# One pipeline for the mixture and the delay screen, with the last stage's weights and coefficients made inside it

## The chip, the cores and the metric

The kernel runs on one core of a Trainium2 chip. The metric is the device time of one execution, in microseconds. An execution is one launch; the profile is one execution more, with its span taken from the first to the last instruction.

## The reference, cut to what matters

The input has 16 samples of 64 channels by 2048 points. A convolution front end turns it into h, 16 tiles of 128 rows by 1024. Four blocks follow, each on a layer norm of h (no gain or bias) and each added to h: attention, a mixture of eight rank-16 experts, the delay average, and a dense layer with eight gated rank-16 adapters.

```python
h = h + attention(layernorm(h))
# mixture: the best expert by x @ route_w.T, weighted by its logit
h = h + out                      # (one_hot * logit * (x @ A)) @ Bw
# delay average, x = layernorm(h)
f = rfft(x); corr = irfft(f * conj(f), n=1024)
weights, delay = top_k(corr, 6)
h = h + sum_k softmax(weights)[k] * x[(i + delay[k]) % 1024]
# dense: x = layernorm(h)
h = h + x @ W.T + b + combined   # combined: softmax over experts of q.k / sqrt(32)
```

The correlation at lag 0 of a normalised row is 1024. Where it leads all other lags by enough, the softmax gives it all the weight in float32, and the delay average of the row is the row itself: h becomes h + layernorm(h). A screen proves this bound for all rows or lets the whole average run.

## The kernel before, in words

h stays in SBUF the whole time (16 tiles, 128x1024 f32). Conv and attention come first and are not touched; attention leaves the coefficients rstd and shift of the mixture's layer norm for tiles 0 to 11. From then on (`middle_stages`, L2064) each stage is a block of its own: all engines meet at its end, and `prime` (L78) opens the semaphores of the next.

**Mixture** (`mixture_stage`, L1361). A loop over 16 tiles on four engines. ACT normalises tile t+2 (L1234) and copies the transposed tile t+1 from PSUM (L1250). PE projects tile t onto 128 adapter rows and 8 logits (L1482, f32), transposes tile t+1 (L1242), makes the output product of tile t-1 (L1474), and transposes the weighted projection wh (L1493). DVE picks the expert in small linked steps (`route_of`, L1432 to L1442) and adds the product to h (L1450). It also takes the statistics of tiles 12 to 15 within the first group. POOL only rounds the screen's tables (L1324); SP loads them.

**Screen** (`screen`, L1504). Again 16 tiles, in four quarters. ACT normalises a row by coefficients taken from h (`ScreenStats`, L1327, a chain of linked steps per quarter on DVE). DVE folds it to sum and difference of its halves (L1558, L1559), PE transposes both (L1643), ACT rounds them (L1604). Per quarter there are four units of a real transform (`dft`, L1657: 8 products of 512 columns each, f32r, two for even and two for odd frequencies), ACT squares real and imaginary parts (L1612), POOL adds them (L1632), PE transforms back to lags 1 to 512 (`correlate`, L1669) and DVE takes each tile's largest (L1565). The smallest lead over all rows against NO_WEIGHT = 150 sets dl_flag (L1587). SP loads qka and bm in this block.

**Delay stage** (`delay_stage`, L1821). Each engine reads the flag. If it is 0, the full average runs (`delay_average`, L1696). Else DVE multiplies ten tiles by 1 + rstd and adds shift (L1857), and ACT does six (L1867).

**Last stage** (`final_stage`, L1876). f32 products are made of three f32r ones, so each weight is split into a rounded high part (ACT, `Weight.high`, L1282) and the rest (`Weight.low`, L1288; POOL has qka and half of w, DVE the other half of w and bm). w has 8 chunks of 1024 columns, qka 5, bm 1. DVE takes the statistics of four tiles at a time (L1145) and makes coefficients in a chain (L1157 to L1161); ACT normalises (L1170) and casts (L1186), DVE makes the low part (L1192). PE does q and k (L2008 to L2010 with qp, ka), waits for w and bm (`ready`), and does the output groups. POOL adds the bias to h (L1929), DVE the product (L1986), SP stores.

What sets the order everywhere is the program order of each engine, written out by hand, with semaphore waits. `Links` (L46) joins small DVE steps: each waits for the one before it.

## Time and profile before

| what | value |
| --- | --- |
| median of 3 runs | 2971.6 us (2968.55 to 2972.6) |
| span of the profiled execution | 2970.8 us, 37847 instructions |
| mean granted TensorE clock | 0.966 of full |
| mixture, screen (in the trace) | 2403.3 to 2493.8, to 2596.0 |
| last stage's block | from 2607.45 to the end |

The page gives no own time of the profiled execution beside its span; the median of the runs is 0.8 us above the span. Times in the trace count from the first instruction. A row of the timeline gives start, length, engine, line and operation; equal neighbours are merged (x16), and the length then runs from the first start to the last end. A matmul's length holds the time until its result is out, so the distance of two starts is the better price. f32 matmuls show as two records each.

### The profile page before, as it was taken

How to read it: one execution, taken by the hardware profiler on the slowest of the kernel's cores; microseconds unless marked ns; L12 is line 12 of the kernel's file. 1: busy time of each engine (PE TensorE's matmuls, PEld its weight loads, DVE VectorE, ACT ScalarE, POOL GpSimd, SP SyncE). 2: the span in 40 equal slices, each digit the busy share in tenths (PEclk: the TensorE clock that was granted, in tenths of full speed). 3: DMA queues.
4: the chain of work that ended last, by engine and by line, in shares of the span. 5: the costliest groups of instructions: out<-in, count | busy, mean ns of one | idle time of the engine just before them, and what ended most of it. 6: DMA issues, size and time to landing. Idle time of an engine off the chain costs nothing. (4 is left out here: it accounts for less than half of the span.)

```text
span 2970.8 us, 37847 instructions
## 1 busy us (share of the span) xinstructions
PE 2775.2 (93%) x13321; PEld 2304.8 (78%) x13321; DVE 1865.8 (63%) x3357; ACT 1003.5 (34%) x2026; POOL 129.9 (4%) x76
## 2 busy tenths in 40 slices
PE   7994899999999999999999999999999887759999
PEld 6772788888788888878888887888888765548888
DVE  4887666667766665777666667766666557462331
ACT  3542333333433333333333333333333334431110
POOL 2110000000000000000000000000000000241100
PEclk9996899999999999999999999999999898879999
DMA  4320322223222222222222222222222111010000
GB/s 110 76 63 0 108 79 78 77 78 94 69 93 79 78 78 78 92 71 88 85 78 78 78 90 66 94 85 78 78 78 92 43 58 43 1 71 29 22 28 29
DMA packets 55469, 207.19 MB, mean 70 GB/s; under 512 B 6784, under 2 KB 7168, under 8 KB 53312
## 3 DMA queue, kind: packets, MB, share of 16 engines
q1 hardware_dynamic: 55360, 205.79, 22.3%
q8 instruction: 63, 1.03, 0.1%
q14 instruction: 46, 0.38, 0.0%
HBM read 197.37 MB, written 8.39 MB: 69 GB/s over the span
## 5 line engine op out<-in xcount | busy, mean ns | idle before, releaser
L1013 PE MATMUL at_proj<-qr_xhi,at_whi 128*128 128x512 f32 x1536 | 615.7, 401 | 11.7 <-DVE at_wlo L884 7.1
L1015 PE MATMUL at_proj<-qr_xhi,at_wlo 128*128 128x512 f32 x1536 | 601.5, 392 | 0.0
L1014 PE MATMUL at_proj<-qr_xlo,at_whi 128*128 128x512 f32 x1536 | 600.0, 391 | 0.0
L754 ACT CAST at_ohi<-at_ov 128x512 fp32r<-128x512 f32 x128 | 75.1, 587 | 847.9 <-PE at_ov L1042 847.9
L1013 PEld LDWEIGHTS at_proj<-qr_xhi,at_whi 128*128 128x128 f32 x1536 | 289.7, 189 | 68.7 <-DVE at_wlo L884 7.7
L1015 PEld LDWEIGHTS at_proj<-qr_xhi,at_wlo 128*128 128x128 f32 x1536 | 289.3, 188 | 63.6
L1014 PEld LDWEIGHTS at_proj<-qr_xlo,at_whi 128*128 128x128 f32 x1536 | 290.2, 189 | 56.7
L1060 PE MATMUL at_out<-at_wohi,at_ohi 128*128 128x512 f32 x1008 | 311.6, 390 | 4.0 <-DVE at_wolo L889 3.0
L1060 PE MATMUL at_out<-at_wohi,at_olo 128*128 128x512 f32 x1008 | 311.3, 390 | 0.0
L1060 PE MATMUL at_out<-at_wolo,at_ohi 128*128 128x512 f32 x1008 | 311.2, 390 | 0.0
L896 DVE TENSOR_TENSOR h<-h,at_out 128x1024 f32 (+1 forms) x126 | 152.7, 1212 | 209.8 <-PE at_out L1060 209.8
L880 DVE TENSOR_TENSOR at_olo<-at_ov,at_ohi 128x512 fp32r<-128x512 f32 x128 | 88.2, 689 | 272.8 <-ACT at_ohi L754 272.8
L884 DVE TENSOR_TENSOR at_wlo<-at_wstage,at_whi 128x1024 fp32r<-128x1024 f32 x192 | 234.1, 1220 | 6.0 <-DMA at_cs<-in_rope_dram 4.5
L1060 PEld LDWEIGHTS at_out<-at_wohi,at_ohi 128*128 128x128 f32 x1008 | 189.8, 189 | 43.9 <-issue 3.3
L1060 PEld LDWEIGHTS at_out<-at_wolo,at_ohi 128*128 128x128 f32 x1008 | 189.8, 188 | 39.6
L1060 PEld LDWEIGHTS at_out<-at_wohi,at_olo 128*128 128x128 f32 x1008 | 189.8, 188 | 39.5
L726 ACT CAST at_whi<-at_wstage 128x1024 fp32r<-128x1024 f32 x192 | 203.5, 1061 | 43.6 <-PE at_proj L1015 40.8
L742 ACT ACTIVATE at_probs<-at_sc,at_ntop 128x128 f32<-128x128 f32 x512 | 182.0, 369 | 102.0 <-DVE at_ntop L858 101.5
L889 DVE TENSOR_TENSOR at_wolo<-at_ostage,at_wohi 128x1024 fp32r<-128x1024 f32 x128 | 153.5, 1220 | 1.4 <-ACT at_wohi L732 1.3
L732 ACT CAST at_wohi<-at_ostage 128x1024 fp32r<-128x1024 f32 x128 | 131.8, 1059 | 34.9 <-DMA at_ostage<-in_w_o_dram 34.8
L843 DVE TENSOR_TENSOR at_q<-at_proj,at_cs 128x512 f32<-128x512 f32 x128 | 88.0, 687 | 84.2 <-PE at_proj L1015 83.7
L1023 PEld LDWEIGHTS at_sc<-at_k,at_q 128*128 128x128 f32 x1024 | 132.0, 192 | 8.1 <-issue 0.7
(244 smaller groups left out, 4250.5 us busy)
## 6 DMA issues: line engine op xcount, KB each, us to landing
at_wstage<-in_w_qkv_dram SPq DMA_DIRECT2D x192, 512.0 KB, 3.6
at_ostage<-in_w_o_dram SPq DMA_DIRECT2D x128, 512.0 KB, 4.4
cv_x<-in_x_dram SPq DMA_DIRECT2D x32, 512.0 KB, 6.5
out_dram<-h SPq DMA_DIRECT2D x16, 512.0 KB, 2.6
fn_w_lo_raw<-in_w_t_dram SPq DMA_DIRECT2D x8, 512.0 KB, 6.8
fn_qka_lo_raw<-in_qka_t_dram SPq DMA_DIRECT2D x5, 512.0 KB, 5.5
sc_fhi_raw<-in_dft_fwd_dram SPq DMA_DIRECT2D x4, 512.0 KB, 7.7
sc_chi_raw<-in_lag_cos_dram SPq DMA_DIRECT2D x2, 512.0 KB, 9.7
```

The costliest lines, as they stand in the source:

```text
L726: act.copy(w_hi[j % 2][:, :], w_stage.buffers[j % 2][:, :]).then_inc(whi_done, 1)
L732: act.copy(wo_hi[:, r, :], o_stage[r % 2][:, :]).then_inc(wohi_done, 1)
L742: last = act.activation(probs[:, r, :], sc[b % 2][:, r * P:(r + 1) * P], ACT.Exp, bias=ntop[:, r:r + 1], scale=SCALE, accum_out=total[:, r ...
L880: dve.tensor_tensor(o_lo[:, :], ov[:, :], o_hi[:, :].bitcast(F32), ALU.subtract).then_inc(olo_done, 1)
L884: dve.tensor_tensor(w_lo[j % 2][:, :], w_stage.buffers[j % 2][:, :], w_hi[j % 2][:, :].bitcast(F32), ALU.subtract).then_inc(wlo_done, 1)
L889: dve.tensor_tensor(wo_lo[:, r, :], o_stage[r % 2][:, :], wo_hi[:, r, :].bitcast(F32), ALU.subtract).then_inc(wolo_done, 1)
L896: dve.tensor_tensor(hb, hb, part, ALU.add).then_inc(added, 1)
L1013: pe.matmul(proj[:, j % 2, :], hi[:, w], x_hi[:, k, :], start=(k == 0), stop=False)
L1014: pe.matmul(proj[:, j % 2, :], hi[:, w], x_lo[:, k, :], start=False, stop=False)
L1015: last = pe.matmul(proj[:, j % 2, :], lo[:, w], x_hi[:, k, :], start=False, stop=(k == KT - 1))
L1023: last = pe.matmul(sc[b % 2][:, r * P:(r + 1) * P], qT[par][:, r, cols], kT[par][:, cols], start=True, stop=True)
L1060: last = pe.matmul(banks[:, c, :], a[:, rows], w[:, r, c * BANK:(c + 1) * BANK], start=first, stop=end)
```

## The change

Mixture and screen become one block and one loop. The full sequence per tile is in the diff. In words:

- The screen works on h itself, not on a normalised copy: tile t-1 is folded as soon as the mixture's product is added, by difference of its halves alone. That leaves the odd frequencies: two transform units per quarter instead of four, four transposes per tile instead of eight, lags 1 to 255 and lag 512 (the negative of the odd part's lag 0). Largest and smallest lag sum are both taken, the lead is scaled by rstd squared at the end, and must lie between 150 and 4096.
- PE's turn, transform and correlation stand at fixed places in the mixture's tile. x_hi of a quarter, power, squares and the banks ri are shared in turn; the last unit uses the banks of the mixture's product.
- The tables are loaded into the place of w's raw chunks and rounded by POOL to half their width; w is loaded after that. qka and bm are loaded at the start and split in tiles 4 to 9 (ACT the high part, POOL the low part).
- Statistics of h are taken per tile in the loop. The last stage's coefficients are derived from them: with g = 1 + rstd, the variance of the updated row is var times g squared. One chain over 16 columns gives scale and bias of all tiles.
- The update h * g + shift moves from the delay stage to ACT in the last stage (`grow`), behind the normalisation of the same tile, and POOL's bias addition waits for it.
- In the last stage ACT casts w and DVE makes all eight low chunks. The statistics and their chains there are gone. If the flag is 0 the average runs as before, then statistics are taken again and all weights are loaded and split again.

The diff, cut to its core (`sc` and `fn` waits that only guard a buffer are left out):

```diff
 class ScreenTables:
+    def load(self, sp):
+        for k in range(KT // 2):
+            cols = slice(k * L, (k + 1) * L)
+            sp.dma_start(self.f_raw[:, cols], self.f_dram[:, cols]).then_inc(self.landed, 16)
+        sp.dma_start(self.c_raw, self.c_dram[:, FT * HALF:2 * FT * HALF]).then_inc(self.landed, 16)
+    def round(self, pool):
+        pool.wait_ge(self.landed, 16 * self.LOADS)
+        for k in range(KT // 2):
+            odd = self.f_raw[:, k * L:(k + 1) * L].rearrange("p (a j s) -> p a j s", a=2, s=2)[:, :, :, 1]
+            pool.tensor_copy(self.f_hi[:, k, :, :], odd).then_inc(self.rounded, 1)
...
 def mixture_stage(...):
+        def units_of(t):
+            q, i = divmod(t, QB)
+            return [(q - 1, i - 2)] if i >= 2 and q >= 1 else []
+        HIGH_AT = {4: (qka, 0), 5: (qka, 1), 6: (qka, 2), 7: (qka, 3), 8: (qka, 4), 9: (bm, 0)}
 # sync
                 tables.load(sp)
+                qka.load(sp)
+                bm.load(sp)
+                sp.wait_ge(tables.rounded, tables.ROUNDS)
+                w.load(sp)
 # gpsimd
                 tables.round(pool)
+                for t in range(NB):
+                    if t in HIGH_AT:
+                        which, c = HIGH_AT[t]
+                        which.low(pool, (c,))
+                    for q, u in units_of(t):
+                        powers(q, u)
+                powers(QUARTERS - 1, 0)
+                powers(QUARTERS - 1, 1)
 # scalar
+                for t in range(NB):
+                    if t >= 2:
+                        high(t - 2)
+                    if t + 1 < NB:
+                        rows.copy(act, t + 1, (t + 1) % 2, pj_done, t)
+                    if t + 2 < NB:
+                        rows.normalize(act, *divmod(t + 2, GROUP))
+                    if t in HIGH_AT:
+                        which, c = HIGH_AT[t]
+                        which.high(act, (c,))
+                    for q, u in units_of(t):
+                        square(q, u, ri)
...
+                    act.copy(wt_sb[t % 2][:, :], wt).then_inc(wt_done, 1)
+                high(LAST - 1)
+                high(LAST)
+                square(QUARTERS - 1, 0, ri)
+                square(QUARTERS - 1, 1, out)
 # vector
+                rows.last_stats(dve, range(GROUP))
+                for t in range(NB):
                     route_of(t)
+                    if t:
                         add(t - 1)
+                        fold(t - 1)
+                        stats.take(dve, t - 1)
+                    if t >= 3:
+                        stats.aggregate(dve, t - 3)
+                    if t >= 9 and t % QB == 1:
+                        tops(t // QB - 2)
+                add(LAST)
+                fold(LAST)
+                stats.take(dve, LAST)
+                tops(QUARTERS - 2)
+                for t in range(NB - 3, NB):
+                    stats.aggregate(dve, t)
...
+                stats.normalizer(dve, link, var, to.rstd, to.shift)
+                link(dve.tensor_scalar(to.gain[:, :], to.rstd[:, :], 1.0, None, ALU.add))
+                link(dve.tensor_tensor(lead[:, :], var, to.gain[:, :], ALU.mult))
+                link(dve.tensor_tensor(lead[:, :], lead[:, :], to.gain[:, :], ALU.mult))
+                stats.normalizer(dve, link, lead[:, :], to.scale, to.bias)
...
+                tops(QUARTERS - 1)
 # tensor
+                def dft(q, u, banks):
+                    pe.wait_ge(hi_done, (q + 1) * QB)
+                    if banks is out:
+                        after(pe, added, NB)
+                    elif u:
+                        pe.wait_ge(squared, q * FT + u)
+                    elif q:
+                        pe.wait_ge(topped, q)
...
+                for t in range(NB):
                     for k in range(KT):
+                        mm = pe.matmul(pj, rows.x[t % 2][:, k, :], ar[:, k * ROUTED:(k + 1) * ROUTED],
...
+                    if t >= 2:
+                        turn(t - 2)
+                    if t + 1 < NB:
                         rows.turn(pe, t + 1)
+                    if t:
+                        outputs(t - 1)
+                    for q, u in units_of(t):
+                        dft(q, u, ri)
+                    if t >= 2 * QB and t % QB == 0:
+                        correlate(t // QB - 2)
                     after(pe, wh_done, t + 1)
...
+                outputs(LAST)
+                correlate(QUARTERS - 2)
+                turn(LAST - 1)
+                turn(LAST)
+                dft(QUARTERS - 1, 0, ri)
+                dft(QUARTERS - 1, 1, out)
                 correlate(QUARTERS - 1)
...
 def delay_stage(...):
-                with dve.Else():
-                    dve.tensor_scalar(gain[:, :], rstd[:, :], 1.0, None, ALU.add).then_inc(gained, 1)
-                    dve.wait_ge(gained, 1)
-                    for t in range(ACT_TILES, NB):
-                        dve.tensor_scalar(h[:, t, :], h[:, t, :], gain[:, t:t + 1], shift[:, t:t + 1],
-                                          ALU.mult, ALU.add)
...
 def final_stage(...):
 # gpsimd
-                qka.low(pool)
-                w.low(pool, range(KT // 2))
-                    after(pool, rows.normed, t + 1)
+                    after(pool, rows.grown, t + 1)
 # scalar
                 def before():
-                    qka.high(act)
                     rows.normalize(act, 0, 0)
                     rows.high(act, 0, 0, out_mm, 0)
                     rows.normalize(act, 0, 1)
                     w.high(act)
-                    bm.high(act)
+                    rows.grow(act, 0, 0)
+                    rows.grow(act, 0, 1)
 # vector
                 def before():
-                    rows.stats(dve, 0, range(GROUP))
                     rows.low(dve, 0, 0)
-                    w.low(dve, range(KT // 2, KT))
-                    bm.low(dve)
+                    w.low(dve)
```

## Rows read from the trace of the kernel before

**Rows 1.** The page's first part: busy time, share of the span, instructions

```profile
PE 2775.2 (93%) x13321; PEld 2304.8 (78%) x13321; DVE 1865.8 (63%) x3357; ACT 1003.5 (34%) x2026; POOL 129.9 (4%) x76
```

**Rows 2.** Windows view by stage: PE, PEld, DVE, ACT, POOL busy (count), clock, DMA

```profile
2403.30:2493.80 90.50, 79.12 (x464) 60.86 (x464) 55.43 (x214) 37.54 (x48) 5.96 (x6) 0.94 0.13 47
2493.80:2596.00 102.20, 74.51 (x321) 58.09 (x321) 56.98 (x132) 49.71 (x48) 20.72 (x16) 0.82 0.09 32
2596.00:2607.45 11.45, 0.00 (x0) 0.00 (x0) 7.50 (x12) 6.92 (x6) 0.00 (x0) 0.51 0.01 2
2607.45:2622.25 14.80, 0.00 (x0) 0.00 (x0) 14.20 (x28) 4.84 (x6) 11.56 (x5) 0.50 0.83 319
2622.25:2647.87 25.62, 12.79 (x65) 12.15 (x65) 16.64 (x7) 13.20 (x14) 17.93 (x6) 0.70 0.00 0
2647.87:2970.80 322.93, 318.47 (x1712) 281.41 (x1712) 93.12 (x243) 44.86 (x91) 33.75 (x14) 0.99 0.07 27
...
2648.00:2651.00 3.00, 3.00 (x8) 2.34 (x9) 2.30 (x8) 1.53 (x3) 0.36 (x1) 0.51 0.03 5
```

**Rows 3.** Timeline of mixture tiles: start, us, engine, line, operation, idle

```profile
2413.70 2.12 PE L1482 MATMUL mx_pj<-mx_ar,mx_x 128*128 128x136 f32 x16 [0.40 <-ACT mx_x L1250]
...
2446.37 2.02 PE L1482 MATMUL mx_pj<-mx_ar,mx_x 128*128 128x136 f32 x16
...
2448.23 1.04 PE L1242 MATMUL mx_tp<-ident,mx_xn 128*128 128x128 f32 x8
...
2448.43 0.17 DVE L1432 COPY mx_logits<-mx_pj 128x8 f32<-128x8 f32 x1 [0.63 <-PE mx_pj L1482]
...
2449.10 1.88 PE L1474 MATMUL mx_out<-mx_b,mx_wt 128*128 128x512 f32 x4
...
2449.63 0.29 DVE L1442 TENSOR_TENSOR mx_wh<-mx_pj,mx_weight 128x128 f32<-128x128 f32 x1
...
2450.93 2.02 PE L1482 MATMUL mx_pj<-mx_ar,mx_x 128*128 128x136 f32 x16
...
2451.14 1.22 DVE L1450 TENSOR_TENSOR h<-h,mx_out 128x1024 f32 x1 [1.22 <-PE mx_out L1474]
```

**Rows 4.** Timeline of DVE work that moves into the loop

```profile
2474.95 1.28 DVE L1344 BATCH_NORM_STATS2 ss_st<-h 128x6 f32<-128x512 f32 x2
...
2490.36 0.16 DVE L55 TENSOR_TENSOR ss_tmp<-rstd 128x4 f32<-128x4 f32 x1
...
2490.56 0.16 DVE L56 TENSOR_TENSOR ss_tmp<-ss_tmp,ss_var 128x4 f32<-128x4 f32 x1
...
2537.89 0.69 DVE L1565 TENSOR_REDUCE sc_top<-sc_co 128x1 f32<-128x512 f32 x1 [0.35 <-PE sc_co L1669]
...
2541.22 0.68 DVE L1559 TENSOR_TENSOR sc_folded<-sc_xn 128x512 f32<-128x512 f32 x1
```

**Rows 5.** Screen: a timeline row of PE, then the tile view of sc_sq

```profile
2515.49 2.10 PE L1657 MATMUL sc_ri<-sc_xhi,sc_fhi 128*128 128x512 f32 x8
...
L1632 POOL TENSOR_TENSOR sc_pw<-sc_sq x16: 1259/1286/1503, 2517.8 to 2586.7; 128x512 fp32r<-128x512 f32 x16
```

**Rows 6.** Timeline: a DVE operation that starts beside a POOL one

```profile
2421.57 2.02 POOL L1324 CAST sc_chi<-sc_chi_raw 128x1024 fp32r<-128x1024 f32 x2
...
2421.64 0.99 DVE L1438 TENSOR_SCALAR mx_weight<-mx_numbers,mx_atf,mx_best 128x8 f32<-128x8 f32 x1
...
2608.58 11.56 POOL L1288 TENSOR_TENSOR fn_qka_lo<-fn_qka_lo_raw,fn_qka_hi 128x1024 fp32r<-128x1024 f32 x5 [20.62 <-ACT fn_qka_hi L1282]
```

**Rows 7.** Final start: timeline; last, the source view of L884

```profile
2627.60 7.68 ACT L1282 CAST fn_w_hi<-fn_w_lo_raw 128x1024 fp32r<-128x1024 f32 x8
...
2632.45 11.99 DVE L1288 TENSOR_TENSOR fn_w_lo<-fn_w_lo_raw,fn_w_hi 128x1024 fp32r<-128x1024 f32 x4 [4.56 <-ACT fn_w_hi L1282]
...
2647.87 0.77 PE L2008 MATMUL fn_out<-fn_w_hi,fn_xhi 128*128 128x512 f32 x1 [9.10 <-DVE fn_bm_lo L1288]
...
L884 DVE TENSOR_TENSOR at_wlo<-at_wstage,at_whi x192: 1212/1218/1227, 310.0 to 2332.7; 128x1024 fp32r<-128x1024 f32 x192
```

More of the change, by code:

```diff
@@ L1277, in load, with load_again, high @@
             sp.dma_start(self.raw[:, self.cols(c)], self.src[:, self.cols(c)]).then_inc(self.landed[c], 16)
-    def high(self, act):
+    def load_again(self, sp, landed):
         for c in range(self.chunks):
+            sp.dma_start(self.raw[:, self.cols(c)], self.src[:, self.cols(c)]).then_inc(landed, 16)
+    def high(self, act, chunks=None):
+        for c in range(self.chunks) if chunks is None else chunks:
             act.wait_ge(self.landed[c], 16)
@@ L1369, in sem @@
             return ctx.enter_context(nc.semaphore(name))
+        f_hi, c_hi = tables.f_hi, tables.c_hi
+        x_hi = [sb(f"sc_xhi{i}", [P, KT // 2, QT], F32R) for i in range(2)]
+        power = sb("sc_power", [P, FT, QT], F32R)
+        rows = RowsAhead(nc, ctx, "mx", h, ident, rstd, shift)
+        b = sb("mx_b", [P, L])
         ar = sb("mx_ar", [P, KT * ROUTED])
-        b = sb("mx_b", [P, L])
-        rows = RowsAhead(nc, ctx, "mx", h, ident, rstd, shift)
+        squares = sb("sc_squares", [P, 2, BANK])
+        folded = [sb(f"sc_folded{i}", [P, HALF]) for i in range(2)]
+        wh = sb("mx_wh", [P, ER])
+        wt_sb = [sb(f"mx_wt{i}", [P, P]) for i in range(2)]
         logits = sb("mx_logits", [P, EXPERTS])
@@ new lines, in square @@
+                def square(q, u, banks):
+                    n = q * FT + u
+                    act.wait_ge(spectrum, n + 1)
+                    if n:
+                        act.wait_ge(powered, n)
+                    act.activation(squares[:, :, :], banks[:, :, :], ACT.Square).then_inc(squared, 1)
+                rows.normalize(act, 0, 0)
+                rows.copy(act, 0, 0, pj_done, 0)
+                rows.normalize(act, 0, 1)
+                for t in range(NB):
[10 more added lines that the diff above has]
+                        square(q, u, ri)
@@ L1689 @@
+                for c in range(2):
+                    last = pe.transpose(fp[0:1, c * P:(c + 1) * P], bound[:, c:c + 1], ident[:, :])
+                last.then_inc(bound_mm, 1)
 TURNS = (["xn", "x_turned", "xT", "x_dft", "x_spectrum", "re2", "im2", "power", "power_0", "power_512",
@@ L1840, in _ @@
                 with sp.If(only_zero(sp) < 1):
+                    for c in range(w.chunks):
+                        sp.wait_ge(w.landed[c], 16)
                     sync(sp)
+                    sp.wait_ge(chain, 2 * NB + stats.AFTER + 2)
+                    for weight in (qka, bm, w):
+                        weight.load_again(sp, again)
+                    sp.wait_ge(again, 16 * (qka.chunks + bm.chunks + w.chunks))
             @block.tensor
@@ L1863, in _ @@
                     scalar(act)
-                with act.Else():
-                    act.wait_ge(gained, 1)
-                    for t in range(ACT_TILES):
-                        act.activation(h[:, t, :], h[:, t, :], ACT.Identity,
-                                       bias=shift[:, t:t + 1], scale=gain[:, t:t + 1])
+                    act.wait_ge(again, 16 * (qka.chunks + bm.chunks + w.chunks))
+                    for weight in weights:
+                        for c in range(weight.chunks):
+                            cols = weight.cols(c)
+                            act.copy(weight.hi[:, cols], weight.raw[:, cols]).then_inc(high, 1)
 DK = 32
```

477 lines of the change are left out of this document (214 added, 263 removed).

## The prediction

> **What bounds the kernel now.** First the page: PE is busy for 93% of the span, DVE for 63% [rows 1]. That is a mean, so I cut the part that the change touches into stages in the windows view [rows 2]. Read the first column (length) against PE's busy time and the clock. Mixture lasts 90.5 us and PE works for 79.1 of them. The screen lasts 102.2 with PE at 74.5 and a mean clock of 0.82. Then come 11.45 us without PE (flag, branch, the rows' update, the next block), 14.8 without PE (statistics and coefficients of the last stage, weight casts), and 25.62 with PE at 12.8 (first transposes and projections, then a wait for split weights). Together 244.6 us, in which PE works for 166. The 322.9 us after them are PE at 318.5: the last stage is bound by PE and the change leaves its matmuls alone. What can be won lies in the 244.6.
>
> Inside mixture the timeline of a steady tile [rows 3] shows PE without a gap: 4.56 us from one projection to the next (1.86 projection, 0.87 eight transposes, 1.83 output product with the transpose of wh). DVE waits 1.22 us before it adds, so it follows PE there. The screen works the same tiles again with normalised copies, and its DVE, ACT and PE wait for one another.
>
> **The change, part by part.**
> I follow T(t), the end of tile t's projection on PE.
>
> *Start.* T(1) is 2413.70 + 2.12, 12.5 us after mixture began [rows 3]. The statistics of tiles 12 to 15 now stand ahead of the first route on DVE: eight bn_stats at 0.62 and some 17 small steps at 0.2 [rows 4], 8.4 us, while the first projection ends 4.56 ahead of T(1), at 7.9, and the second waits for ACT anyway [rows 3]. SP now issues qka and bm (6) right after the tables and then waits for POOL's six roundings before the 8 loads of w; only these stand behind that wait, and they have the whole loop to land. POOL's roundings read every second column and are half as wide as its casts now. Cost 0 for all of it.
>
> *The loop, T(1) to T(15), by PE's list.* Fourteen tiles at 4.56: 63.8. Four transposes of the folded row for 13 tiles, each half of the 0.87 for eight: 5.7. A transform unit is 8 products with 512 columns, 1.9 us (2.10 less the drain) [rows 5]; where before there were 16 units, 8 are left, and five fall before T(15): 9.5. A correlation is 8 products with 256 columns, half a unit: two of them, 1.9. Sum 80.9.
>
> *DVE's list per tile.* Route 1.5 and add 1.14 as now [rows 3]; fold 0.6, two bn_stats 1.2 and an aggregate with its memset 0.25, from [rows 4]: 4.7 to 4.9, against PE's 5.0 in tiles without a unit and 6.9 with one. So the cover is thin in half of the tiles. The top of a quarter (two reductions over 1020 columns, 1.2 each by the 0.69 for 512, and a copy: 2.5) is in front of the next quarter's first unit, because both use the bank pair ri; PE does its other work first and waits about 1.1, twice: 2.2. ACT has room: 37.5 busy now [rows 2], and sixteen half-width casts at 0.6, six weight casts and eight squares at 1.0 bring it to 61 of 125. Gone are its sixteen normalisations for the screen, one fold of two, and three quarter-wise coefficient chains.
>
> *The shared-port stalls.* In [rows 6] a DVE operation of 8 columns that normally takes 0.29 starts 0.07 after a POOL cast and takes 0.99: it ends as the cast ends. POOL gets 14 operations beside the loop and its tail: five splits of qka and one of bm at 2.3 (11.56 for five) [rows 6], eight power sums at 1.29 [rows 5]. Bounds: none meets DVE, 0; each holds it for its full length, 24. Splits start late in a tile, behind ACT's cast, when DVE is in bn_stats, and half of the sums fall in tiles where PE has 2 us more work than DVE. I take 3, near the lower end. The Trainium skill (SBUF — State Buffer, Who interferes with whom) says that a DVE instruction with two SBUF inputs contends with a GpSimd one that reads SBUF, and that the lock lasts for the whole instruction. By that rule the folds, the 33 chain steps and the power sums collide wherever they meet, which is the upper bound; the held row above is of this kind.
>
> T(15) is then 12.5 + 80.9 + 2.2 + 3 = 98.6 us after the start, against 81 now.
>
> *Tail to the flag.* After T(15) PE has 0.4 + 1.8 + 1.9, then waits for ACT's square (1.0, as its 1024-column casts in [rows 7]) and copy: output 15 ends at 7.3. DVE: add 8.5, fold 9.1, bn_stats 10.3, top of quarter 2 at 12.8; that frees ri. From there two chains run side by side. PE: two units, square, power sum, square, power sum (one squares buffer, so in turn), correlation: 12.8 + 1.9 + 1.0 + 1.3 + 1.0 + 1.3 + 1.0 and handovers is 20, or 22 at the low clock. DVE: three aggregates and 33 linked steps at 0.2 (variance to final scale and bias, now derived instead of measured): 20.2, plus 1 for the two sums. Both near 21. Then top 2.5, eleven small steps with one pair of transposes 3: 26.5. In all 125.1 us from start to flag where now there are 192.7.
>
> *Between flag and last stage.* Now 11.45, of which 7.5 is DVE's update of ten tiles [rows 2]. The update moves into the last stage (ACT, 1.24 per tile, in 20 us tiles in which ACT works for 3: hidden). Left: branch, block change, 3.95.
>
> *Last stage's start.* No statistics: the 14.8 goes to 0, as scale and bias are ready. From the first normalisation to the first output product it was 25.62. PE's own work on this way ends 9.10 earlier [rows 7], at 16.5: the floor. DVE now splits all eight chunks of w. The first cast starts 5.35 after the normalisation and ends at 6.4. DVE took 3.0 for each of four while POOL did the others; alone it takes 1.22 (192 cases) [rows 7]. So 6.4 + 9.7 = 16.1, plus 2 because POOL's bias addition of tile 0 starts under the last chunks: 18.0. Bounds: 16.5 and, if all eight cost 3.0, 30.4. As PE hardly waits, the stretch at clock 0.51 from 2648 [rows 2] should go: 1.2 less.
>
> **Sum.** Now 244.6; after 125.1 + 3.95 + 0 + 18.0 = 147.05. Saved 97.5 + 1.2 = 98.7. Span 2970.8 - 98.7 = 2872.1. The page gives the span of the profiled execution; the median of the runs is 0.8 above it, and I add that: 2873. 0.2% (6 us) is about what can be told from no change.
>
> **Rivals.**
> *DVE sets the pace of the loop.* In tiles without a unit DVE has 4.9 of 5.0. If POOL's operations hold it at their full length, every hold is paid: 24 instead of 3, 2894. For it: [rows 6]. Against: the splits' place in the tile and the room in unit tiles.
> *The last stage starts no sooner than its weights.* If DVE splits at 3.0 as in [rows 7], the first output product waits until 30.4: 2885. For it: the row itself. Against: POOL has no splits left there, and two additions can hold DVE for 5 us at most.
> *Better than the list.* No holds, tops under PE's queue, PE's tail at full clock, branch quicker without an else side: 3 + 2 + 2 + 1, 2865.
> *The other side: the new screen says no.* It judges by odd frequencies only, with half of the zero lag's weight: the lead must be 150 where the zero lag of a normalised row is 1024 in full and 512 in the odd half. Then the delay average runs for all rows. Its price from rows: 29 transposed blocks and 58 f32 products with 512 columns per tile, 53 us at 1.83 a pair [rows 3], 3 for transposes, some 26 for DVE and ACT in one chain: 82 a tile, 1300 in all, 2873 + 1300 = 4170. It decides at one row below 150. Against: off-lag sums of a row of 1024 near-random numbers are some 32 wide, their largest odd half near 130, which leaves about 380.
>
> **How the numbers follow.** Forecast 0.66, with its own range 2865 to 2885 (holds 0 to 12, tail clock 0 to 4, branch 2 either way). DVE's pace 0.18, late weights 0.10, better than the list 0.04, the screen says no 0.02. The range must hold 8 in 10 and take in the bounds of the holds and of the split: 2862 to 2896. Every case but the last is faster by far more than 6 us: faster 0.97, same 0.01, slower 0.02.
>
> **What would show it.** Right: in the profile after, PE without gaps in tiles 2 to 15 at 5.0 or 6.9; DVE's fold near 0.7 and only a few at over 1.3; the flag near 2528; the first last-stage matmul some 6 us after its block starts; the eight w splits at 1.2. Wrong: DVE waiting for nothing while PE waits for wh; many DVE rows of 8 or 512 columns at 1.5 to 2.5 us beside POOL; the flag later than 2540; any transform of the delay average in the trace; more than the present 322.9 from the first output product of the last stage to the end.

## The result, and the profile after

The median is 2879.36 us (2876.24 to 2880.92, 4 runs) against 2972.1 in the same session: ratio 0.969, 95% interval 0.9679 to 0.9702. The forecast was 2873 with 2862 to 2896: right in sign and range, 6.4 us too low. One of the four runs of experiment i_early below took 5750.57 us at a mean clock of 0.53; it is left out, and every other run named here was undisturbed. The profiled execution has a span of 2879.2 us, 37181 instructions and a mean clock of 0.974.

The windows view of the kernel after, one row per stage as in [rows 2]: window, length, busy time (and instructions) of PE, PEld, DVE, ACT and POOL, granted clock, DMA share, GB/s.

```profile
2403.30:2422.00 18.70, 10.79 (x51) 10.19 (x52) 9.25 (x37) 5.81 (x6) 3.07 (x6) 0.63 0.92 347
2422.00:2506.00 84.00, 82.57 (x516) 64.78 (x515) 66.85 (x210) 49.66 (x65) 22.06 (x11) 1.00 0.14 56
2506.00:2535.20 29.20, 17.26 (x64) 11.79 (x62) 22.87 (x77) 4.98 (x7) 4.41 (x4) 0.75 0.00 0
2535.20:2542.03 6.83, 0.00 (x0) 0.00 (x0) 0.03 (x1) 0.00 (x1) 0.00 (x0) 0.50 0.03 7
2542.03:2557.67 15.64, 11.90 (x65) 11.23 (x65) 10.40 (x9) 13.55 (x15) 1.27 (x1) 0.69 0.11 34
2557.67:2879.20 321.53, 317.08 (x1712) 280.38 (x1712) 70.71 (x159) 61.74 (x106) 38.15 (x16) 1.00 0.07 27
```

The stages are: start to T(1); loop to T(15); tail to the flag; flag to the last stage; its first normalisation to the first output product; the rest. Against the sum:

| stage | forecast | measured | off by |
| --- | --- | --- | --- |
| start to T(1) | 12.5 | 18.7 | +6.2 |
| T(1) to T(15) | 86.1 | 84.0 | -2.1 |
| tail to the flag | 26.5 | 29.2 | +2.7 |
| flag to the last stage | 3.95 | 6.83 | +2.9 |
| statistics | 0 | 0 | 0 |
| first normalisation to first output product | 18.0 | 15.64 | -2.4 |
| from there to the end | 322.9 - 1.2 = 321.7 | 321.5 | -0.2 |

The errors add to +7.1, which is 2879.2 - 2872.1. That is closer than the terms deserve: three came out 11.8 longer in all, three 4.7 shorter, and part of the closeness is luck. The large mechanism is as forecast: PE works for 82.6 of the loop's 84 us at full clock, and the 14.8 us of statistics are gone. Three stages came out longer, and each has a cause of its own.

**Start.** A group of the lines view from 2403 to 2422 (busy and mean ns, then idle time before it with its releaser), and two PE rows of the timeline:

```profile
L1225 DVE BATCH_NORM_STATS2 mx_st<-h 128x6 f32<-128x512 f32 x8 | 4.8, 679 | 5.9 <-DMA mx_numbers<-in_experts_dram 5.9
...
2417.93 0.48 PE L1708 MATMUL sc_fp<-ident,mx_wh 128*128 128x128 f32 x1 [5.19 <-DVE mx_wh L1558]
...
2418.20 3.83 PE L1687 MATMUL mx_pj<-mx_ar,mx_x 128*128 128x136 f32 x16
```

DVE stands for 5.9 us in front of the statistics, waiting for a table (the expert numbers) that only the routing behind them needs. The statistics then hold the first route back, PE waits 5.19, and the projection after the gap runs at half clock: 3.83, not 2.12 as in [rows 3]. The granted clock was 1.00 in the transposes before the gap (2411.7 to 2412.8) and is 0.51 from 2417.9 to 2422.0.

**A tile without a transform unit**, one of the first. Timeline, from one projection to the next:

```profile
2429.32 0.59 PE L1641 MATMUL mx_out<-mx_b,mx_wt 128*128 128x512 f32 x1
...
2429.85 2.02 PE L1687 MATMUL mx_pj<-mx_ar,mx_x 128*128 128x136 f32 x16
...
2429.95 1.22 DVE L1565 TENSOR_TENSOR h<-h,mx_out 128x1024 f32<-128x1024 f32 x1 [0.75 <-PE mx_out L1641]
...
2431.20 0.69 DVE L1573 TENSOR_TENSOR sc_folded<-h 128x512 f32<-128x512 f32 x1
...
2431.95 0.42 PEld L1653 LDWEIGHTS sc_fp<-ident,sc_folded 128*128 128x128 f32 x4 [0.28 <-DVE sc_folded L1573]
...
2432.44 1.04 PE L1242 MATMUL mx_tp<-ident,mx_xn 128*128 128x128 f32 x8
...
2433.32 1.88 PE L1641 MATMUL mx_out<-mx_b,mx_wt 128*128 128x512 f32 x4
```

PE's idle time is small but it stands in a ring: output product, DVE's add and fold, transposes of the folded row, transposes of the next row, next output product. It comes round every 5.29 us in tiles 2 to 5, where the list had 5.0, and the first tile with a unit takes 7.14. After that the list holds: 6.84 with a unit, near the 6.9 forecast, 5.0 without (tiles 9 and 13), and 7.83 where reductions stand in front of the unit (tiles 10 and 14).

**A split of POOL beside DVE**, the first of six. The fold has started 0.19 before it and keeps its 0.69, and the statistics beside it (1.28 for two, as elsewhere) are not lengthened either:

```profile
2441.78 0.69 DVE L1573 TENSOR_TENSOR sc_folded<-h 128x512 f32<-128x512 f32 x1
2441.97 2.72 POOL L1292 TENSOR_TENSOR fn_qka_lo<-fn_qka_lo_raw,fn_qka_hi 128x1024 fp32r<-128x1024 f32 x1 [22.02 <-ACT fn_qka_hi L1286]
2442.39 1.28 DVE L1374 BATCH_NORM_STATS2 ts_st<-h 128x6 f32<-128x512 f32 x2
```

All sixteen folds take 0.69; here it is POOL that gives way, as its 2.72 will show against the 2.37 of an experiment below. Two steps of DVE are held in the loop, both by a power sum of POOL and both until it ends: 0.75 and 0.73 for 0.29.

```profile
2455.23 1.28 POOL L1489 TENSOR_TENSOR sc_power<-sc_squares 128x512 fp32r<-128x512 f32 x1
...
2455.79 0.75 DVE L1554 TENSOR_SCALAR mx_weight<-mx_numbers,mx_atf,mx_best 128x8 f32<-128x8 f32 x1
```

Neither costs time: the projections around them stand 6.85 apart (a tile with a unit) and 5.94 (one with a correlation), as they do in tiles 11 and 12, where nothing is held. The 3 us booked for holds in the loop were not needed.

**Tail.** Timeline after T(15) (2506.1):

```profile
2519.02 3.75 PE L1667 MATMUL sc_ri<-sc_xhi,sc_fhi 128*128 128x512 f32 x8 [2.85 <-DVE sc_zero L1583]
...
2522.57 2.81 PE L1667 MATMUL mx_out<-sc_xhi,sc_fhi 128*128 128x512 f32 x8
...
2523.91 1.31 DVE L53 TENSOR_SCALAR ts_var<-ts_var 128x16 f32<-128x16 f32 x1
...
2523.91 1.28 POOL L1489 TENSOR_TENSOR sc_power<-sc_squares 128x512 fp32r<-128x512 f32 x1 [11.39 <-ACT sc_squares L1516]
...
2526.51 1.30 POOL L1489 TENSOR_TENSOR sc_power<-sc_squares 128x512 fp32r<-128x512 f32 x1 [1.32 <-ACT sc_squares L1516]
...
2527.87 2.08 PE L1677 MATMUL sc_ri<-sc_chi,sc_power 128*128 128x256 f32 x8 [2.50 <-POOL sc_power L1489]
...
2530.05 1.22 DVE L1581 TENSOR_REDUCE sc_most<-sc_ri 128x4 f32<-128x1020 f32 x1 [1.37 <-PE sc_ri L1677]
...
2535.03 0.20 DVE L1632 TENSOR_SCALAR dl_flag<-sc_bound_row 1x1 int32<-1x1 f32 x1
```

PE waits 2.85 for the reductions that free its banks, and runs its next unit in 3.75 instead of 2.1: the granted clock from 2519.0 to 2522.6 is 0.50. The correlation ends 23.8 us after T(15), where the forecast had 20, or 22 at the low clock.

**Last stage:**

```profile
2542.03 1.24 ACT L1943 ACTIVATE fn_xn<-h,rt_bias,rt_scale 128x1024 f32<-128x1024 f32 x1 [15.59 <-PEq L80]
...
2548.44 9.17 DVE L1292 TENSOR_TENSOR fn_w_lo<-fn_w_lo_raw,fn_w_hi 128x1024 fp32r<-128x1024 f32 x8 [0.85 <-ACT fn_w_hi L1286]
...
2556.40 5.82 POOL L2000 TENSOR_TENSOR h<-h,fn_bias 128x1024 f32 x2 [28.59 <-ACT h L1949]
2557.67 0.50 PE L2077 MATMUL fn_out<-fn_w_hi,fn_xhi 128*128 128x512 f32 x1
```

The eight splits take 9.17 (four took 11.99, [rows 7]), and PE passes to its output products without the wait of 9.10. Nothing is to spare: the last split ends at 2557.61, PE's own work in front of the product at 2557.57.

### The profile page after: what moved, and what is told of

Its sections match the earlier page's. It is cut to its first block and busy times, and to the rows that moved or that the text cites. A ratio compares the mean times of both kernels' runs of the same rounds, so it can differ in the third digit from the quotient of the medians.

```text
span 2879.2 us, 37181 instructions
## 1 busy us (share of the span) xinstructions
PE 2728.6 (95%) x13162; PEld 2269.5 (79%) x13162; DVE 1802.0 (63%) x3214; ACT 980.1 (34%) x2012; POOL 109.0 (4%) x65
## 5 line engine op out<-in xcount | busy, mean ns | idle before, releaser
L1013 PE MATMUL at_proj<-qr_xhi,at_whi 128*128 128x512 f32 x1536 | 615.0, 400 | 13.2 <-DVE at_wlo L884 8.9
L884 DVE TENSOR_TENSOR at_wlo<-at_wstage,at_whi 128x1024 fp32r<-128x1024 f32 x192 | 234.2, 1220 | 7.4 <-DMA at_cs<-in_rope_dram 5.8
L843 DVE TENSOR_TENSOR at_q<-at_proj,at_cs 128x512 f32<-128x512 f32 x128 | 88.0, 688 | 84.6 <-PE at_proj L1015 84.1
```

The lines of the kernel that those rows point to most:

```text
L884: dve.tensor_tensor(w_lo[j % 2][:, :], w_stage.buffers[j % 2][:, :], w_hi[j % 2][:, :].bitcast(F32), ALU.subtract).then_inc(wlo_done, 1)
L1013: pe.matmul(proj[:, j % 2, :], hi[:, w], x_hi[:, k, :], start=(k == 0), stop=False)
```

## The experiments

Attention ends up to 3 us earlier or later from one trace to the next (the mixture's first transposes stand at 2402.67 in a_numbers and at 2405.66 in f_shortbody), which moves a whole trace. Stage lengths are therefore compared beside the ratios. They are measured in each trace from the first transposes of the mixture: to the start of projection 1, to the start of projection 15, to the end of the flag's write, to the first normalisation, to the first output product. The ratio's interval is about 0.0015 to either side, 4.5 us.

| kernel | median us | ratio | to proj. 1 | loop | tail | flag to norm. | norm. to product | sum |
| --- | --- | --- | --- | --- | --- | --- | --- | --- |
| after | 2879.4 | 0.969 | 13.4 | 85.9 | 31.1 | 6.8 | 15.6 | 152.9 |
| a_numbers | 2872.3 | 0.9671 | 9.1 | 84.1 | 30.2 | 6.5 | 15.6 | 145.5 |
| b_banks | 2878.8 | 0.9691 | 13.8 | 85.6 | 29.8 | 6.5 | 16.0 | 151.7 |
| c_order | 2874.6 | 0.9676 | 13.3 | 83.9 | 31.3 | 6.5 | 15.8 | 150.7 |
| d_three | 2871.3 | 0.9666 | 8.7 | 82.9 | 29.8 | 6.4 | 16.2 | 143.8 |
| e_nobranch | 2874.6 | 0.9674 | 13.4 | 86.0 | 31.2 | 2.1 | 15.9 | 148.5 |
| f_shortbody | 2876.6 | 0.9678 | 12.9 | 86.2 | 31.2 | 3.6 | 15.7 | 149.7 |
| g_update | 2886.0 | 0.971 | 13.7 | 85.8 | 31.1 | 10.9 | 17.3 | 158.7 |
| h_halfstats | 2876.2 | 0.968 | 13.2 | 84.2 | 29.3 | 6.4 | 15.6 | 148.7 |
| i_early | 2884.0 | 0.971 | 13.4 | 90.5 | 30.2 | 6.7 | 15.6 | 156.4 |
| j_wsplit | 2890.5 | 0.9731 | 14.0 | 85.6 | 31.0 | 6.8 | 22.3 | 159.7 |
| l_derive | 2883.0 | 0.9706 | 13.2 | 86.0 | 31.2 | 10.0 | 15.7 | 156.0 |
| k_best | 2871.7 | 0.9667 | 9.0 | 81.6 | 27.1 | 10.0 | 15.6 | 143.3 |

Two stages also differ between kernels that are the same there, because the clock comes back sooner or later. Where the first projection's start was not edited, the interval from projection 1 to projection 2 is 5.8 to 6.7 us. Where the tail was not edited it lasts 31.0 to 31.3 in five traces, and 30.2 in a_numbers and i_early. In those two PE waits the same 2.86 us ahead of its unit, but the unit takes 2.68 and 2.95 instead of 3.75. So a difference of up to 1 us in the tail, or in a loop that begins at half clock, need not come from an edit.

**a_numbers**

```diff
-                dve.wait_ge(numbers_in, 16)
                 rows.last_stats(dve, range(GROUP))
+                dve.wait_ge(numbers_in, 16)
```

> In the changed kernel DVE waits for mx_numbers (a transfer) before the statistics of tiles 12 to 15, idles 5.9 us, and the first route starts at 2416.07 instead of 2411.44; PE idles 5.2 us and runs the second projection at 1.2 GHz (3.83 instead of 2.12 us). Here the wait stands behind the statistics. Theory: that misplaced wait is the whole of the late start, so the first wh comes near 2413.4, the second projection ends near 2415.9 instead of 2422.0, and the span falls by 6 us, to 2873. Rival: the statistics and their chain (8.1 us) or the loads, now 14 more on the queue, make the start late by themselves; then DVE still reaches the first route after 2414 and less than 2 us are saved (2878).

```profile
2411.46 0.33 PE L1708 MATMUL sc_fp<-ident,mx_wh 128*128 128x128 f32 x1 [0.80 <-DVE mx_wh L1558]
2411.77 2.12 PE L1687 MATMUL mx_pj<-mx_ar,mx_x 128*128 128x136 f32 x16
```

PE's wait falls from 5.19 to 0.80 and projection 1 runs at full clock. The way to its end (13.4 + 3.8 against 9.1 + 2.1) is 6.0 us shorter. One wait, one line too early, was worth 6 us, where the forecast was off by 7 in all.

**b_banks**

```diff
-                dft(QUARTERS - 1, 0, ri)
-                dft(QUARTERS - 1, 1, out)
+                dft(QUARTERS - 1, 0, out)
+                dft(QUARTERS - 1, 1, ri)
```

(ACT's two squares change their banks in the same way, and the second unit waits for the reductions of quarter 2 in place of the first.)

> The last quarter's first transform unit goes to the banks of the mixture's product and the second one to ri, so the first need not wait for DVE's reductions of quarter 2 (PE waits 2.85 us there and then runs the unit in 3.75 us at the low clock). Theory: in the tail PE's chain and DVE's chain of 33 small steps run side by side and end within 1.4 us of each other, so an earlier PE gains only that gap: the flag comes 1 to 1.5 us earlier (span 2878), and DVE's last reductions then start right behind its chain, without idle time. Rival: PE's chain alone sets the tail; then 3.5 to 4 us are saved (2875).

```profile
2515.89 2.14 PE L1669 MATMUL mx_out<-sc_xhi,sc_fhi 128*128 128x512 f32 x8 [0.68 <-ACT sc_xhi L1507]
...
2518.08 2.06 PE L1669 MATMUL sc_ri<-sc_xhi,sc_fhi 128*128 128x512 f32 x8
...
2519.20 1.28 DVE L52 TENSOR_SCALAR rt_rstd<-ts_tmp 128x16 int32<-128x16 int32 x1
...
2521.77 1.17 DVE L57 SCALAR_TENSOR_TENSOR rt_rstd<-ts_tmp,rt_rstd 128x16 f32<-128x16 f32 x1
...
2522.96 1.90 PE L1679 MATMUL sc_ri<-sc_chi,sc_power 128*128 128x256 f32 x8 [2.83 <-POOL sc_power L1489]
...
2527.79 1.22 DVE L1581 TENSOR_REDUCE sc_most<-sc_ri 128x4 f32<-128x1020 f32 x1
```

Both units run at full clock and the correlation ends 19.7 us after T(15) instead of 23.8, but the tail gains only 1.3, little more than it varies by itself: DVE comes from its own chain of coefficients, with no wait, at 2527.79. Two of its steps of 0.17 were held for 1.28 and 1.17 beside POOL's sums. The two chains of the forecast were near each other, as it said: remove one and the other is the bound.

**c_order**

```diff
                     if t >= 2:
-                        turn(t - 2)
                     if t + 1 < NB:
                         rows.turn(pe, t + 1)
+                    if t >= 2:
+                        turn(t - 2)
```

(ACT's copies change places in the same way.)

> PE transposes the next normalised row before the folded one, and ACT copies in the same order. Theory: in tiles without a transform unit the period 5.29 us is a ring through two engines: output product 1.83, addition 1.22, fold 0.69, folded transposes 0.44, row transposes 0.88, then the next output product. With the row transposes ahead of the folded ones the ring is 4.4 us and PE's own list (5.0) sets the period: 0.29 us less in each of some seven tiles, 2 us in all (2877). Rival: DVE's list (4.9 plus semaphore steps) sets the period; then it stays at 5.2 to 5.3 and nothing is saved (2879).

```profile
2433.56 0.69 DVE L1573 TENSOR_TENSOR sc_folded<-h 128x512 f32<-128x512 f32 x1
...
2434.07 1.04 PE L1242 MATMUL mx_tp<-ident,mx_xn 128*128 128x128 f32 x8
...
2434.95 0.60 PE L1653 MATMUL sc_fp<-ident,sc_folded 128*128 128x128 f32 x4
```

The projections now start every 4.99 to 5.00 us in the tiles without a unit: the list's value. The fold is no longer waited for, and the loop is 2.0 shorter. Of these, 1.5 are the ring's (tiles 2 to 6, 0.29 each); the other 0.5 lie between projections 1 and 2 (5.82 for 6.37), where h_halfstats shows the same without this edit.

**d_three** has the three edits together.

> All three edits together. Theory: 6.2 + 2 + 1.4 = 9 to 10 us less than the changed kernel, 2870 us. If they cover each other, the sum of the three single gains is not reached: 2873.

The stages give 9.1 less than after, near the sum of the three (7.4 + 1.2 + 2.2 = 10.8 by the table). Its median is 1 us from that of a_numbers, within the intervals: nearly all that can be measured came with the first edit.

**e_nobranch** leaves out the block with the branch.

```diff
-        delay_stage(nc, average, h, after_it, flag, spare, qka, bm, w)
```

> The block with the flag's branch is left out, so the delay average can't run in this kernel; everything else is as in the kernel after. It prices the stretch from DVE's last write of the flag to the first normalisation of the last stage, 6.83 us in the kernel after where the sum had 3.95. Theory 'the branch costs it' (each engine loads the flag and jumps past the unused average): the stretch falls to about 2 us, one change of block, and the time by 4.5 to 5, ratio to the kernel before 0.967. Rival 'the last stage's block is what starts slowly': the stretch stays above 5 us and the time is that of the kernel after, 0.969.

**f_shortbody** keeps the branch and cuts its bodies.

```diff
                 with pe.If(only_zero(pe) < 1):
-                    tensor(pe)
+                    pe.sem_inc(again, 1)
```

(the same on SP, DVE and ACT)

> The branch on the flag is kept, but the bodies behind it are cut to one semaphore increment per engine, so the delay average, its statistics and the reload of the weights are left out. Theory 'the jump over a long body costs' (the engines go on at a far place of the program): the stretch from flag to last stage falls from 6.83 to about 4 us, time 2.5 to 3 less than the kernel after. Rival 'loading and testing the flag costs, however long the body': the stretch stays within 0.5 of 6.83 and the time within 1 us of the kernel after.

**g_update** moves the update back.

```diff
+                with dve.Else():
+                    for t in range(6, NB):
+                        dve.tensor_scalar(h[:, t, :], h[:, t, :], after_it.gain[:, t:t + 1],
+                                          after_it.shift[:, t:t + 1], ALU.mult, ALU.add)
```

(the same on ACT for six tiles; `grow` and the two products with the gain are taken out)

> The update h times g plus shift goes back into the branch's other side (ten tiles on DVE, six on ACT, as in the kernel before) and the last stage normalises the updated rows; scale and bias are no longer multiplied by the gain. It prices the moving of the update. Sum of the prediction: the update cost 7.5 of 11.45 us, so flag to last stage is 6.83 + 7.5 = 14.3 us and the time 7.5 more than after, less 1 us or so for the first tile's update that no longer stands in front. Rival 'part of the 6.83 is there only because nothing covers it' (the kernel before had 11.45 in all): the stretch is 11 to 12 us and the time 4 to 5 more than after.

The flag's write ends at 2533.69 in e, 2536.04 in f and 2533.91 in g. One row of e, one of f, the rest of g:

```profile
2535.82 1.24 ACT L1943 ACTIVATE fn_xn<-h,rt_bias,rt_scale 128x1024 f32<-128x1024 f32 x1 [10.87 <-PEq L80]
```

```profile
2539.67 1.24 ACT L1912 ACTIVATE fn_xn<-h,rt_bias,rt_scale 128x1024 f32<-128x1024 f32 x1 [12.33 <-PEq L80]
```

```profile
2535.96 7.32 DVE L1914 TENSOR_SCALAR h<-h,rt_gain,rt_shift 128x1024 f32<-128x1024 f32 x10 [2.05 <-issue]
...
2544.79 1.24 ACT L1949 ACTIVATE fn_xn<-h,rt_bias,rt_scale 128x1024 f32<-128x1024 f32 x1 [2.50 <-PEq L80]
...
2548.32 4.70 POOL L2006 TENSOR_TENSOR h<-h,fn_bias 128x1024 f32 x2 [21.82 <-DMA fn_bias<-in_bias_dram]
...
2551.20 10.85 DVE L1292 TENSOR_TENSOR fn_w_lo<-fn_w_lo_raw,fn_w_hi 128x1024 fp32r<-128x1024 f32 x8 [0.85 <-ACT fn_w_hi L1286]
...
2562.11 0.50 PE L2079 MATMUL fn_out<-fn_w_hi,fn_xhi 128*128 128x512 f32 x1 [2.08 <-DVE fn_w_lo L1292]
```

The stretch is 2.1 without a branch, 3.6 with one that has short bodies and 6.8 with the long ones: 3.2 us hang on the length of what is jumped over (or on where the program goes on). The other 1.5 hold the load and test and also the end of one block more, since e has left out the block itself.

One thing beside the 3.2 is in the traces. The DMA view, asked for this stretch, lists loads of instructions (queues q8 and q14): in the kernel after three of them 2.4 to 2.8 us after the flag and one at 6.4, just ahead of the last stage. f has one in all, at 3.0, and e one, at 1.8. In g the three stand at 2.2 to 2.8 and the fourth at 5.4, where DVE and ACT are still at the update. That three more loads come with the long bodies is shown; that an engine waits for them is not.

With the update behind the branch, DVE works from 2.05 to 9.4 after the flag and the last stage starts 1.5 later. 10.9 - 7.3 leaves 3.6, near the 3.95 of the kernel before: the update had covered 3.2 us that show once it is gone. Which engine's way through the branch they are, no row tells. The rival that expected 11 to 12 for the stretch was the nearer one. That the time rose by 6.7 us, near the 6.5 of the first theory, is chance: 1.7 of it came behind the stretch.

The kernel g shows one thing more. POOL's bias additions need not wait for `grow` there, so they run beside DVE's splits, which take 10.85 instead of 9.17, and PE waits 2.08 for them. That is the plus of 2 that the forecast had; the change itself removed it by making the addition wait.

**h_halfstats** takes statistics from half of each row.

```diff
-        for c in range(2):
+        for c in range(1):
             last = dve.bn_stats(self.st[:, t, c, :], self.h[:, t, c * BANK:(c + 1) * BANK])
```

> In the loop each tile's statistics are taken of the first half of its row alone, one bn_stats instead of two, which takes 0.6 to 0.7 us a tile off DVE's list (the last stage's rows are then normalised with the statistics of half a row). Theory 'a ring sets the pure tiles' (output product, add, fold, folded transposes, row transposes, output product, 5.29 us): the statistics lie beside the ring, the pure tiles stay at 5.29, and the time moves only in the tail, by at most 1 us. Rival 'DVE's list sets the pace' (my 18% case): pure tiles fall towards 4.7 and the time by 0.6 times 14, 8 us.

Tiles without a unit stay at 5.29: DVE does not set the pace, and that rival falls. What did change is the tile in which a quarter's reductions stand behind the statistics: 7.22 against 7.83, twice, and the tail by 1.8, where the same order holds. There PE waits for the reductions, so each bn_stats ahead of them counts in full: 0.61 a time in the loop, and in the tail PE's wait falls from 2.85 to 2.27. The rest of the tail's 1.8 is mostly the clock, which came back sooner (the two units take 3.57 and 2.00 instead of 3.75 and 2.81). I had expected at most 1 us of it.

**i_early** has ACT's weight cast ahead of the normalisation.

```diff
-                    if t + 2 < NB:
-                        rows.normalize(act, *divmod(t + 2, GROUP))
                     if t in HIGH_AT:
                         which, c = HIGH_AT[t]
                         which.high(act, (c,))
+                    if t + 2 < NB:
+                        rows.normalize(act, *divmod(t + 2, GROUP))
```

> In tiles 4 to 9 ACT casts the weight chunk ahead of the normalisation, not behind it, so POOL's split of 2.7 us starts about 1.2 us earlier in the tile, before DVE's fold instead of 0.19 us behind its end. All six splits of the kernel after lie behind a fold and no fold is longer than 0.69. Theory 'the place in the tile saved the loop' (a DVE operation of two SBUF inputs that meets a POOL operation is held until it ends): the folds of these tiles take 1.5 to 2.5 us, the fold is part of the ring that sets the pure tiles, so each costs 0.8 to 1.8, and the time rises by 4 to 9 us. Rival 'POOL's splits don't hold DVE in this loop': folds stay at 0.69, time within 1 us of the kernel after.

```profile
2440.54 2.37 POOL L1292 TENSOR_TENSOR fn_qka_lo<-fn_qka_lo_raw,fn_qka_hi 128x1024 fp32r<-128x1024 f32 x1 [20.98 <-ACT fn_qka_hi L1286]
2441.48 1.97 DVE L1573 TENSOR_TENSOR sc_folded<-h 128x512 f32<-128x512 f32 x1
2443.38 1.27 DVE L1374 BATCH_NORM_STATS2 ts_st<-h 128x6 f32<-128x512 f32 x2
```

All six folds of these tiles take 1.96 to 2.01, the ten others 0.69: 7.7 us of holds, of which 4.6 come out in the loop. The fold ends 0.54 after POOL does. The expectation had the splits of the kernel after behind the end of the fold; by its rows they start 0.19 behind the fold's start. So it is not distance that saves the fold but being first: there POOL takes 2.72, here, ahead of the fold by 0.94, 2.37.

**j_wsplit**

```diff
+                w.low(pool, range(KT // 2))
                 pool.wait_ge(bias_in, 16)
...
-                    w.low(dve)
+                    w.low(dve, range(KT // 2, KT))
```

> The last stage's split of w goes back to half on POOL and half on DVE. Theory 'POOL's absence made DVE's splits cheap' (3.0 us each before with POOL beside it, 1.15 now): DVE's four take 10 to 12 us again, POOL's four about 11, the last is ready later than PE wants it, and the first output product comes about 19 to 20 us after the first normalisation instead of 15.64; time 3 to 4.5 us more than after. Rival 'two engines are quicker than one' : the split ends at half its time, but since PE never waited for it the time is that of after, within 1 us.

```profile
2548.06 11.37 POOL L1292 TENSOR_TENSOR fn_w_lo<-fn_w_lo_raw,fn_w_hi 128x1024 fp32r<-128x1024 f32 x4 [20.70 <-ACT fn_w_hi L1286]
...
2551.81 11.98 DVE L1292 TENSOR_TENSOR fn_w_lo<-fn_w_lo_raw,fn_w_hi 128x1024 fp32r<-128x1024 f32 x4 [4.64 <-ACT fn_w_hi L1286]
...
2563.85 0.79 PE L2078 MATMUL fn_out<-fn_w_hi,fn_xhi 128*128 128x512 f32 x1 [6.78 <-DVE fn_w_lo L1292]
```

Two engines need 15.7 us for the eight chunks (2548.06 to 2563.8), one needs 9.17. PE waits 6.78, and its granted clock is 0.50 for the next 4.0 us, and the rest is 3.2 longer (324.8 from this product to the end, against 321.5): 1.9 of it PE's longer busy time (319.0 against 317.1), 1.3 idle time. The price is 6.6 + 3.2; I had expected 3 to 4.5, without DVE's wait of 4.64 for the fifth cast and without the clock.

**l_derive and k_best** put the derivation of scale and bias behind the branch, in its other side on DVE; k_best also has d_three's edits and the reductions ahead of the statistics.

```diff
                         fold(t - 1)
+                    if t >= 9 and t % QB == 1:
+                        tops(t // QB - 2)
                         stats.take(dve, t - 1)
...
+                with dve.Else():
+                    own(dve.tensor_scalar(to.gain[:, :], to.rstd[:, :], 1.0, None, ALU.add))
...
+                    kept.normalizer(dve, own, grown_var[:, :], to.scale, to.bias)
```

> The last stage's coefficients are derived behind the branch, on its other side, instead of ahead of the flag: some 20 linked steps of DVE, 4.3 us, leave the tail. In the tail of the kernel after, DVE waited 1.37 us for PE's last correlation all the same, so the theory (PE, ACT and POOL in turn set the end of the tail, and the jump past the unused average has room for DVE's work, as the update showed) says: flag as before, within 0.5 us, flag to first normalisation 7 to 7.8 instead of 6.8, time 0 to 1 more than after. Rival 'DVE's list sets the tail': the flag comes 2 to 4 us earlier and the time falls by as much. Rival 'work behind the branch is not hidden': the stretch grows to 10.5 to 11 and the time rises by 3 to 4.

> The three edits of d_three, the reductions of a quarter ahead of the tile's statistics, and the coefficients derived behind the branch. By the theory that PE's chain takes the tail over once DVE's list is shorter: the loop's two tiles with reductions go from 7.8 to 7.2 (1.2 in all), T(15) to the flag goes from 27.8 to about 24.7, flag to first normalisation rises by at most 1, so 2871.3 less 1.2 and 3.1 plus 1 is 2868. Rival: the tail is as long as in d_three and the time 2870 to 2872.

In l_derive the tail is as long as in after (31.2 and 31.1) although DVE has some 20 steps less: it now waits 7.46 for the correlation, which settles that PE, ACT and POOL in turn set the tail of the kernel after, and that DVE's two held steps there cost nothing. In k_best, with the banks exchanged, the shorter list counts: loop 1.3 and tail 2.7 below d_three, near the 1.2 and 3.1 forecast. With the reductions in front, POOL's power sum now comes ahead of the fold in two tiles, by 0.18 in the first, and these folds take 1.64 and 1.65. But both kernels lose time behind the branch, 3.2 us against after and 3.6 against d_three. The first linked step of k_best:

```profile
2525.72 0.17 DVE L1912 TENSOR_SCALAR rt_gain<-rt_rstd 128x16 f32<-128x16 f32 x1 [4.33 <-issue]
```

DVE arrives 4.3 us after the flag, not 2.05 as in g_update, so the 3.9 us of steps add to the way and the stretch is 10.0. My theory that they would be covered is wrong; the second rival was nearly right. Why the same jump took 2.05 in g_update and in the kernel before and 4.3 here, I can't say. The loads of instructions come at 2.2 to 2.6 in these two kernels, before DVE's first step, and in g_update behind it; whether DVE waits for one of them is not shown. And what the two have in common against these (work on ACT behind the same branch, no waits in DVE's body) was not tried alone. k_best equals d_three within the intervals, as its rival's 2870 to 2872 said, but not for the rival's reason: the tail did get shorter, and the branch took it back; both beat the kernel after, and a_numbers does so with one line.

## Why the prediction was right, and where it was off

- **Start, 12.5 against 18.7.** The failed term, and the largest. The step counted 8.4 us of statistics from the start of the mixture, and asked only what they were ahead of, not what they stood behind. DVE's wait for the expert numbers had been harmless as long as only the route followed it. Price: 4.3 us of time and 1.7 for the half clock after it (a_numbers).
- **The loop by PE's list, 80.9.** Right in kind. The list is the pace only if no ring is longer than it; in the first tiles the ring through DVE's fold was, by 0.29 in each of five (c_order). The stretch came out at 84.0 against 86.1 mainly because the 3 us of holds were not paid and the ring cost 1.5.
- **Tops, 2.2.** The size is right: a tile with reductions takes 7.83 where its neighbour takes 6.85, so 2.0 for the two. The make-up is not. PE's wait right before the unit is only 0.45; the rest is lost ahead of it, where two statistics stand in front of the reductions that I had not put in the chain. One bn_stats less gives 0.61 a tile (h_halfstats), the reductions in front of both 0.56 (k_best).
- **Holds, 3.** Two small ones in the loop, 0.9 us together, and two in the tail; none cost anything in the kernel after. The mechanism is real: 7.7 us when the split starts 1.2 us earlier (i_early). The rival at 2894 was wrong for the reason given, the splits' place in the tile. The Trainium skill (SBUF — State Buffer, Who interferes with whom) says that a DVE instruction with two SBUF inputs contends with a GpSimd one that reads SBUF, and, of DVE's two-port modes, that whoever issues first has the shared pair for its whole length; it gives issue order as what decides. The folds of i_early (1.97 for 0.69) and the splits of the kernel after (2.72 for 2.37) agree. It lists tensor_scalar as able to contend too, and the held steps of 128x16 (1.31, 1.28) agree; the held row of [rows 6] is such a TENSOR_SCALAR too, with one tensor as its input. The kernel before had the dearest case, in the statistics of its last stage, beside POOL's splits of qka [rows 6]. Three steps of 0.17 took 2.26 each there; two of them:

```profile
2613.32 2.26 DVE L51 TENSOR_SCALAR fn_tmp<-fn_var 128x4 int32<-128x4 int32 x1
...
2617.91 2.26 DVE L53 TENSOR_SCALAR fn_var<-fn_var 128x4 f32<-128x4 f32 x1
```

So 6.3 of the 14.8 us that the change took away were holds. The bn_stats just before them ran beside the first splits without one (4.84 for eight, as in the start of the kernel after, without POOL); bn_stats and the reductions over sc_ri were held in no trace here.
- **Tail, 26.5 against 29.2.** The top of quarter 2 ended 12.8 after T(15), as forecast. Behind it the chain over PE was cold: 3.75 and 2.8 for the two units and 2.08 for the correlation. I had named the low clock (22 instead of 20) and not taken it. b_banks shows the remedy and its limit.
- **Branch, 3.95 against 6.83.** The failed term here. I subtracted the update's 7.5 from a stretch in which it ran beside something else. With the update gone, 3.2 us show that it had covered, and they go with the long bodies behind the branch (e, f, g); which engine spends them stays open.
- **First output product, 18.0 against 15.64.** The splits took 1.15 each against 1.22, and POOL's addition came only under the last of them, because it waits for the update of its tile; the plus of 2 was priced from rows in which nothing made it wait. The floor of 16.5 was none: PE's own work in front of the product ended at 15.54, because its clock was full from 9.5 us after the normalisation, and in the kernel before only from 11.6. The cold stretch behind the first product did go: 321.5 from there, forecast 321.7.

## What to carry to other kernels

When work moves ahead of a step, look at the waits that already stand in front of that place in the engine's program, not only at what comes behind. When a stage with two parts loses one, the rest is not the difference of the times: price what the removed part covered. And on two engines that share a port, who comes first decides: a split that starts 0.2 us behind the fold costs the fold nothing, one that starts ahead of it holds the fold until it has ended.

## What the runs showed that I had not expected

- Held steps need not be the long ones: a step of 0.17 took 1.28 beside POOL, and a hold costs nothing where the engine would wait anyway.
- Two engines on one split are slower than one: 15.7 us for eight chunks on POOL and DVE, 9.17 on DVE alone.
- A branch around code that does not run costs 1.5 us with one instruction inside and 4.7 with the delay average inside (3.6 - 2.1 and 6.8 - 2.1), the end of its block included.
- A pause of PE is paid twice: 3.83 for 2.12 after a wait of 5.2 us in the start, 3.75 for 2.1 after 2.85 in the tail, and 1.9 us more of busy time after 6.8 in j_wsplit. The second price is not fixed: the same wait in the tail, 2.86, was followed by a unit of 2.68 in a_numbers and 2.95 in i_early.
